# A conditioned transformer block on Trainium2: the first norm's row made on TensorE, and x loaded ahead of the value weights

## The reference

```python
def rmsnorm(x, w):
    return x * jax.lax.rsqrt(jnp.mean(x * x, axis=-1, keepdims=True) + EPS) * w
def film(x, cond, w, b):
    scale, shift = jnp.split(cond @ w + b, 2, axis=-1)
    return x * (1.0 + scale[:, None, :]) + shift[:, None, :]
h = film(rmsnorm(x, norm1_w), cond, film1_w, film1_b)
Q, K, V = h @ q_w + q_b, h @ k_w + k_b, h @ v_w + v_b
attn = softmax(einsum('bnd,bmd->bnm', Q, K) * D ** -0.5)
x = x + (einsum('bnm,bmd->bnd', attn, V) @ proj_w + proj_b)
h = film(rmsnorm(x, norm2_w), cond, film2_w, film2_b)
return x + gelu(h @ mlp_w1 + mlp_b1) @ mlp_w2 + mlp_b2
```

## Time and profile before

| | |
|---|---|
| median of 3 timed runs | 1751.23 us (1750.7 to 1751.26) |
| the profiled execution | 1747.36 us |
| its span in the trace | 1745.6 us |
| TensorE busy | 1738.3 us, 100% of the span |
| VectorE, ScalarE, GpSimd busy | 74%, 51%, 11% |
| mean granted TensorE clock | 1.000 |
| HBM traffic | 226 GB/s over the span |

### The profile page before, as it was taken

How to read it: one execution, slowest core, us unless ns; L and a number is a source line. 1 busy time by engine, 2 the same in 40 slices (tenths; PEclk the granted TensorE clock), 3 DMA queues, 4 the chain that set the end, 5 groups by cost and what they waited for, 6 DMA issues and landing times.

```text
span 1745.6 us, 23156 instructions
## 1 busy us (share of the span) xinstructions
PE 1738.3 (100%) x8274; PEld 1461.1 (84%) x8274; DVE 1287.8 (74%) x1767; ACT 890.5 (51%) x1498; POOL 198.8 (11%) x206
## 2 busy tenths in 40 slices
PE   9999999999999999999999999999999999999999
PEld 7888888888888888888888888888888888888887
DVE  5878888566765887688588768858876885885477
ACT  6645445554544654455465445546544554653344
POOL 1467676000000000000000000000000000000000
PEclk9999999999999999999999999999999999999999
DMA  9478778832237678777867866886786678677676
GB/s 343 155 260 301 249 301 278 279 104 87 67 133 219 191 265 268 204 230 264 241 193 265 268 204 229 265 241 192 265 267 204 227 268 241 193 241 242 193 224 209
DMA packets 201969, 395.81 MB, mean 227 GB/s; under 512 B 23936, under 2 KB 28032, under 8 KB 199808
## 3 DMA queue, kind: packets, MB, share of 16 engines
q1 hardware_dynamic: 201632, 393.81, 69.8%
q0 software_dynamic: 224, 0.53, 0.1%
HBM read 331.25 MB, written 62.98 MB: 226 GB/s over the span
## 4 chain that ended last, share of the span: by engine, by line
PE 98%; DMA 1%; DVE 0%; SPq 0%; ACT 0%; issue 0%; POOL 0%; DVEq 0%
PE psum L707 35%; PE psum L727 23%; PE psum L595 14%; PE psum L735 12%; PE psum L635 3%; PE psum L636 3%; PE psum L640 3%; PE psum L677 3%; DMA norm_row<-rs_scratch 0%; PE psum L668 0%; DMA x_tok<-x_dram 0%; DMA rs_scratch<-rstd 0%; PE psum L609 0%; PE psum L752 0%; ACT x_tok L847 0%; DVE h L1105 0%
## 5 line engine op out<-in xcount | busy, mean ns | idle before, releaser
L707 PE MATMUL psum<-op_hi_P,ring 128*128 128x512 f32 x1792 | 551.8, 389 | 0.0
L727 PE MATMUL psum<-stage_hi,ring 128*128 128x512 f32 x1784 | 440.6, 389 | 0.0
L707 PEld LDWEIGHTS psum<-op_hi_P,ring 128*128 128x128 f32 x1792 | 336.2, 188 | 69.6
L727 PEld LDWEIGHTS psum<-stage_hi,ring 128*128 128x128 f32 x1784 | 334.9, 188 | 69.5
L942 ACT CAST stage_hi<-x 128x1024 fp32r<-128x1024 f32 x224 | 235.4, 1055 | 235.2 <-PE psum L727 223.0
L707 PE MATMUL psum<-op_lo_P,ring 128*128 128x512 f32 x896 | 348.6, 389 | 0.0
L1333 DVE TENSOR_TENSOR stage_lo<-x,stage_hi 128x1024 fp32r<-128x1024 f32 x224 | 273.5, 1224 | 72.4 <-ACT stage_hi L942 72.3
L926 ACT ACTIVATE x<-x,vecs 128x512 f32<-128x512 f32 x192 | 138.1, 723 | 278.3 <-DVE x L1320 278.2
L735 PE MATMUL psum<-stage_lo,ring 128*128 128x512 f32 x892 | 238.4, 389 | 0.0
L707 PEld LDWEIGHTS psum<-op_lo_P,ring 128*128 128x128 f32 x896 | 168.2, 188 | 34.8
L735 PEld LDWEIGHTS psum<-stage_lo,ring 128*128 128x128 f32 x892 | 167.5, 188 | 34.7
(11 more groups left out here) (167 smaller groups left out, 2242.1 us busy)
## 6 DMA issues: line engine op xcount, KB each, us to landing
ring<-wu_scratch SPq DMA_DIRECT2D x448, 256.0 KB, 3.0
ring<-wd_scratch SPq DMA_DIRECT2D x448, 256.0 KB, 2.9
x_tok<-x_dram SPq DMA_DIRECT2D x16, 1024.0 KB, 11.6
xT_in<-xT_dram SPq DMA_DIRECT2D x16, 1024.0 KB, 8.9
x2T_scratch<-xT_in SPq DMA_DIRECT2D x32, 512.0 KB, 4.3
hn<-x2T_scratch SPq DMA_DIRECT2D x32, 512.0 KB, 5.2
xres<-x2T_scratch SPq DMA_DIRECT2D x32, 512.0 KB, 5.3
out_dram<-xres SPq DMA_DIRECT2D x31, 512.0 KB, 4.4
```

Source lines behind the costliest of these rows:

```text
L707: mm = pe.matmul(to, wt, b, start=q in FRESH and t == 0, stop=t == len(steps) - 1, skip_group_check=True)
L727: mm = pe.matmul(bank(q, dt), a[:, dt, part, :], stage_hi[r][:, e, :], start=q in FRESH and ss == 0 and e == 0 and part == 0, stop=False, ...
```

## The change

The first group's row is no longer taken through HBM. VectorE multiplies the identity by `rstd` into `row_diag` (128x512: column 4q + j holds rstd[q, j] on partition q and zero elsewhere), splits it into `diag_hi` and `diag_lo`, and TensorE multiplies a matrix of ones by both, which puts the row on all partitions of bank 2, `row0`. These two matmuls stand between chunks 1 and 2 of the film product. `scale_x(0)` reads `row0` in PSUM. It moves ahead of the low parts of chunk 1, and SP's load of x ahead of all value weights. GpSimd's store and load of row 0 go; those of row 1 stay.

```diff
--- before.py
+++ after.py
@@ -163,6 +163,8 @@
         probs, pT_sb = at(88, "probs", [P, GB, P]), at(90, "pT_sb", [P, TOK])
         key_bias = at(92, "key_bias", [P, TOK])
         key_halves = at(94, "key_halves", [P, TOK], F32R)
+        row_diag = at(88, "row_diag", [P, TOK])
+        diag_hi, diag_lo = at(90, "diag_hi", [P, TOK], F32R), at(92, "diag_lo", [P, TOK], F32R)
         xT_in = [at(kb, f"xT_in{r}", [P, KD, TOK]) for r, kb in enumerate((168, 128, 176))]
         x_tok = at(160, "x_tok", [P, GB, D])
         norm1_row = [at(184 + 2 * r, f"norm1_row{r}", [P, TOK]) for r in range(2)]
@@ -192,6 +194,7 @@
         gv = [ps[2 * j] for j in range(KD)]
         score, pT, out_ps = ps[1], ps[3], (ps[5], ps[7])
         film_ps = [ps[0].rearrange("p (j b) -> p j b", j=2 * KD), ps[7].rearrange("p (j b) -> p j b", j=2 * KD)]
+        row0 = ps[2]
         vp_ps = [ps[2 * c + 1] for c in range(KD)]
         score_b = score.rearrange("p (b t) -> p b t", b=GB)
 
@@ -247,6 +250,7 @@
         vp_hi_done, vp_lo_done = sem("vp_hi_done"), sem("vp_lo_done")
         wk_loaded, wq_loaded, wpT_loaded = (sem(n) for n in ("wk_loaded", "wq_loaded", "wpT_loaded"))
         bias_cols_done = sem("bias_cols_done")
+        diag_done, row0_full = sem("diag_done"), sem("row0_full")
         first_rstd_stored, first_row_loaded = sem("first_rstd_stored"), sem("first_row_loaded")
         one_plus_done, film1_bias_done, bq_bk_done = (sem(n) for n in ("one_plus_done", "film1_bias_done", "bq_bk_done"))
         film_full, film_read = sem("film_full"), sem("film_read")
@@ -397,9 +401,8 @@
             sp.dma_start(vecs[:], cols).then_inc(loaded["vecs"], 16)
             for k in range(KD):
                 sp.dma_start(f1w_sb[:, k, :], f1w[tokens(k), :]).then_inc(f1w_loaded[k], 16)
+            load_xT(0)
             for k in range(KD):
-                if k == 2:
-                    load_xT(0)
                 sp.dma_start(wvT_sb[:, k, :], wvT[tokens(k), :]).then_inc(vp_loaded[k], 16)
                 sp.dma_start(wp_sb[:, k, :], wp[tokens(k), :]).then_inc(vp_loaded[k], 16)
             load_x_tok(1)
@@ -559,13 +562,13 @@
                 nc.gpsimd.tensor_tensor(both[:, :, :, 1, :], src, both[:, :, :, 0, :].bitcast(F32),
                                         ALU.subtract).then_inc(w_split, 1)
 
-            for m in range(2):
-                norm1(m)
-                pool.wait_ge(rstd_done, m + 1)
-                nc.gpsimd.dma_start(rs[m].rearrange("(p j) -> p j", p=P), rstd[:]).then_inc(first_rstd_stored, 16)
-                pool.wait_ge(first_rstd_stored, 16 * m + 16)
-                nc.gpsimd.dma_start(norm1_row[m][:], rs[m:m + 1, :].broadcast_to([P, TOK])
-                                     ).then_inc(first_row_loaded, 16)
+            norm1(0)
+            pool.wait_ge(diag_done, 1)
+            norm1(1)
+            pool.wait_ge(rstd_done, 2)
+            nc.gpsimd.dma_start(rs[1].rearrange("(p j) -> p j", p=P), rstd[:]).then_inc(first_rstd_stored, 16)
+            pool.wait_ge(first_rstd_stored, 16)
+            nc.gpsimd.dma_start(norm1_row[1][:], rs[1:2, :].broadcast_to([P, TOK])).then_inc(first_row_loaded, 16)
             norm1(2)
             for n in range(GROUPS):
                 if n < CHUNKS:
@@ -765,6 +768,10 @@
             pe.wait_ge(prod_lo, 1)
             pe.wait_ge(loaded["condT"], 16)
             for k in range(KD):
+                if k == 2:
+                    pe.wait_ge(diag_done, 3)
+                    pe.wait_ge(prod_lo, 2)
+                    product(row0, [(ones_r[:], diag_hi[:]), (ones_r[:], diag_lo[:])], row0_full)
                 pe.wait_ge(f1w_loaded[k], 16)
                 for j in range(2 * KD):
                     mm = pe.matmul(film_ps[0][:, j, :], f1w_sb[:, k, tokens(j)], condT_sb[:, k, :],
@@ -1097,13 +1104,16 @@
 
             def scale_x(m):
                 dve.wait_ge(xT_loaded[m % 3], 16 * (m // 3) + 16)
-                if m < 2:
-                    dve.wait_ge(first_row_loaded, 16 * m + 16)
+                row = row0 if m == 0 else norm1_row[m % 2][:]
+                if m == 0:
+                    dve.wait_ge(row0_full, 1)
+                elif m == 1:
+                    dve.wait_ge(first_row_loaded, 16)
                 else:
                     dve.wait_ge(row_loaded[m % 2], 16 * (m // 2))
                 for k in range(KD):
                     dve.scalar_tensor_tensor(by_batch(h[m % 2][:, k, :]), by_batch(xT_in[m % 3][:, k, :]), ROOT_D,
-                                             by_batch(norm1_row[m % 2][:]), ALU.mult, ALU.mult).then_inc(x_scaled, 1)
+                                             by_batch(row), ALU.mult, ALU.mult).then_inc(x_scaled, 1)
 
             def modulate(m, k):
                 dve.wait_ge(x_scaled, KD * m + k + 1)
@@ -1231,12 +1241,21 @@
                 dve.tensor_scalar(one_plus[:, f, :], col(b)[:, 0:KD], 1.0, None, ALU.add).then_inc(one_plus_done, 1)
             dve.wait_ge(one_plus_done, 1)
             dve.tensor_tensor(film1_bias[:], one_plus[:, 0, :], col("n1"), ALU.mult).then_inc(film1_bias_done, 1)
-            for c in range(KD):
+            dve.wait_ge(rstd_done, 1)
+            dve.wait_ge(ones_r_done, 1)
+            dve.tensor_tensor(row_diag.rearrange("p (q t) -> p q t", t=GB), ident[:].unsqueeze(2).broadcast_to([P, P, GB]),
+                              rstd[:].unsqueeze(1).broadcast_to([P, P, GB]), ALU.mult).then_inc(diag_done, 1)
+            qk_low(0)
+            dve.wait_ge(diag_done, 1)
+            dve.tensor_copy(diag_hi[:], row_diag[:]).then_inc(diag_done, 1)
+            dve.wait_ge(diag_done, 2)
+            dve.tensor_tensor(diag_lo[:], row_diag[:], diag_hi[:].bitcast(F32), ALU.subtract).then_inc(diag_done, 1)
+            for c in range(1, KD):
                 qk_low(c)
             dve.wait_ge(weights_lo, 2 * KD)
             for k in range(KD):
                 weights_low(1, k, wvT_sb, wv_hi, wv_lo, wp_sb, wp_hi, wp_lo)
-                if k == 1:
+                if k == 0:
                     scale_x(0)
             dve.wait_ge(film_read, 1)
             modulate(0, 0)
```

## The result

The changed kernel takes 1745.57 us, the median of 22 timed runs (1745.12 to 1752.03); the kernel before, timed beside it, 1749.61 (22 runs, 1747.41 to 1751.38). The ratio is 0.9978, 95% interval 0.9973 to 0.9984: 3.8 us less (2.8 to 4.7). The forecast was 1.9 us less. The profiled execution, however, does just what was forecast: it takes 1745.62 us, with a span of 1743.8 after 1745.6, so 1.8 less.

What follows compares the result with a forecast made beforehand. TensorE was taken as busy throughout except one hole, the most the change could win. 2.66 + 0.07 - 0.54 - 0.31 = 1.9 us less, from the median 1751.23 to 1749.3 us; range 1747.9 to 1751.2.

Steps and rivals of the forecast that it cites:

- the hole and its restart: TensorE's wait for `wp_lo` at chunk 2 of the value weights, 2.66 us plus 0.07 restart, would go.
- the row matmuls: Two added 128x512 matmuls inside the film product on TensorE, on the path, would cost 0.54 us.
- chunk 1's wait and restart: TensorE would wait 0.24 us at chunk 1 of the value weights, plus 0.07 for the restart: 0.31 us.
- g's first product: TensorE's first product of g, behind the value weights, would start at 36.2 to 36.7 us instead of 38.29.
- Landing of chunk 0: Value weights' chunk 0, behind 1 MB more of x, would land at 21.8 us instead of 18.6; bounds 21.2 and 22.6.
- Scalings from PSUM: VectorE's four scalings of x reading row 0 from PSUM would cost nothing extra; upper bound 0.26 us.
- rival 5: VectorE's scalings take 750 ns each from PSUM instead of 684; gain 1.6 us, time 1749.6; chance 8%.
- `h_hi` and `key_halves`: TensorE's needs behind the value weights: no new waits; h's casts end by 35.3 us, key row has 0.97 us slack.
- the three diagonal operations: VectorE's row_diag, diag_hi and diag_lo would finish by 19.55 us, 1.5 us before TensorE asks; cost 0.
- the difference carries over: The 1.9 us saved in the profiled span, all in the first 36 us, would come off the timed median 1751.23 unchanged.
- that it passes 2.7 is excluded by the waits: In the more-than-the-hole rival (gain 2.3 us, chance 10%), TensorE's waits cap the whole gain at 2.7 us.
- The moves of the load and of the scalings: x's load ahead of value weights delays chunk 0; scalings ahead of chunk 1's low parts remove chunk 2's hole; 0.31 us wait.

Runs made afterwards that it cites:

- after_again: The changed kernel, unedited, timed once more beside others on one chip; ratio 0.9973 to the kernel before.
- hole_filled: The kernel before with 11 extra unread 128x512 matmuls between chunks 1 and 2 of the value weights; 1748.07 us, ratio 0.9992.
- filled_again: The same kernel as hole_filled, on another chip; 1748.50 us, ratio 0.9993 to the kernel before.
- hole_doubled: The kernel before with four more VectorE operations of 128x512 behind the scalings, to lengthen TensorE's hole; 1752.38 us, ratio 1.0022.
- hole_late: The changed kernel with a TensorE hole in the MLP, a wait for two spare GpSimd operations; 1749.57 us, ratio 1.0002 to the kernel before.
- row_only: The kernel before with only the row made on TensorE, row_diag behind `qk_low(0)`; load of x and scalings unmoved; 1744.87 us over 12 executions.
- best: The changed kernel with scalings back behind chunk 1's low parts and row_diag behind `qk_low(0)`; ratio 0.9982 to the kernel before, repeated 0.9976.
- hole_half: The kernel before with 5 extra matmuls between chunks 1 and 2 of the value weights; 1750.02 us, ratio 1.0005.
- wait_after_heavy: row_only with five spare VectorE operations behind the scalings, so TensorE waits for chunk 2; 1745.62 us, ratio 0.9975 to the kernel before.

## Why the prediction was wrong

**Right: where TensorE's time goes.** Against the profiled span the sum holds term by term: the hole and its restart, 2.73, gone; the row matmuls 0.55 (forecast 0.54); chunk 1's wait and restart 0.28 + 0.08 (0.31); g's first product at 36.55 (36.2 to 36.7); the span 1743.8 (1743.7). The film product's late start is in this sum at nothing, by luck, as the next paragraph says. Landing of chunk 0: ScalarE took it up at 21.98 (21.8 assumed between 21.2 and 22.6). Scalings from PSUM at no extra cost: right, and rival 5 falls with the rule of the Trainium skill behind it (2.48 us for four, after 2.50). `h_hi` and `key_halves` made no wait.

**Partly wrong: the three diagonal operations at a cost of 0.** The cover was reckoned with `rstd` at 15.36. It came at 16.12, and TensorE had reached the film product 0.49 earlier, so `qk_low(0)` behind row_diag cost 0.36 us of idling, 0.52 from start to start. The earlier arrival made up for it, which was luck and no part of the forecast; in after_again the same wait was 0.8 us. The three operations do cost something: with row_diag behind `qk_low(0)` the kernel is 0.7 us faster. The cast took 0.42 us.

**The step that failed: "the difference carries over" from the profiled execution to the median.** The forecast saw that the profiled execution lay 3.9 us below the median of the timed ones and took this for something around the kernel that the change leaves alone: "for reasons outside it". By the experiments it was the clock's fall behind the very hole that the change closes, a term that the sum put at nothing: a hole of 2.66 us, a lower clock in 85 of 105 executions, 2.3 or 3.5 us each. Without a fall the kernel before takes 1747.3 and the changed one 1745.5; those 1.8 us are what the sum was made for (1.9). The profile before showed a clock of 1.00 and I wrote "its clock granted in full"; true for that execution, and not for four of five others. It is shown by hole_filled and filled_again (the hole filled in part or nearly, nothing saved: 1 of 22 falls), hole_doubled (7 of 7, and the trace of one) and hole_late (6 of 11, at another place). Of a gain above the hole the forecast said "that it passes 2.7 is excluded by the waits": the loss behind a hole is in no list of waits. Of the 3.7 us between the forecast of 1749.3 and the measured 1745.57, some 2 are this term. The other 1.6 are the base: the three runs it was taken from (1750.7 to 1751.26) lie where the times at 0.998 do, while all 22 have a median of 1749.61; so most of that is the clock too.

**Forecast as needed, and not.** The moves of the load and of the scalings, on which most of the sum's uncertainty hung, were not needed: each undone alone costs nothing, and row_only, with both undone, is no slower than best at 1.000.

**Open.** No trace of the kernel before with a fall was caught; that it lies behind the hole rests on the experiments. What a hole must be to cost the clock is not settled. With 1.4 us in the profiled execution it fell in 7 of 11 (hole_half), with 1.8 us in 1 of 10 (wait_after_heavy), with 2.2 us in 1 of 11 (filled_again), and best, with none, in 7 of 18; so length alone does not order them, and the length in the other executions is not known. The two executions of the changed kernel at 0.996, 6.4 us longer, are not explained, and none of best's falls is in a trace.

## What to carry to other kernels

A hole of TensorE costs its length and, in part of the executions, a stretch at half clock behind it; closing one of 2.7 us was worth 3.8 and 4.7 us in the changed kernel's two series of runs, 5.1 and 5.6 in row_only's. Compare the profiled execution's time with the median of the timed ones before a sum is made against it: where it lies outside the others, list the granted clock of each execution and ask which kind the profile caught. Whether more slack at the loads protects the clock is suggested by row_only (0 of 12 falls) against best (7 of 18), and not shown.

## What was not expected of the hardware

The same program runs at a mean clock of 1.000, 0.999 or 0.998, all three on each of the four chips used in the experiments, with medians of 1747.3, 1749.6 and 1750.9 us. TensorE's clock fell in 7 of 11 executions of a kernel whose profiled execution waits 1.4 us at chunk 2 (hole_half). Useless matmuls in a hole cost nothing measurable, or even gain: 1748.2 us with them (22 executions), 1750.0 without (105), with ratios whose intervals just reach 1.
